# The last add of a windowed-ratio kernel: by an accumulating DMA issued from POOL, in place of a POOL instruction

## The chip, the cores and the metric

The kernel runs on one core of one Trainium2 chip. The metric is the device time of one execution in microseconds (us); lower is better. The core's engines are PE (TensorE), DVE (VectorE), ACT (ScalarE), POOL (GpSimd) and SP (SyncE, which issues the loads and stores here). Sixteen DMA engines move the data.

## The reference

x is 2 x 128 x 128 x 192 in float32 (batch, rows, w, channels). It is group-normalised (32 groups of 6 channels, statistics over rows, w and the group), a ratio of window sums is formed from the result, and the ratio is added to x.

```python
WINDOW = (1, 5, 20)
def _L0_conv_ref(x):
    w0, w1, w2 = WINDOW
    s = box_sum(box_sum(x, 1, w0), 2, w1)
    num = box_sum(s * s, 3, w2)
    d = box_sum(box_sum(box_sum(x * x, 1, w0), 2, w1), 3, w2)
    c0 = box_sum(jnp.ones((x.shape[1],), x.dtype), 0, w0)
    c1 = box_sum(jnp.ones((x.shape[2],), x.dtype), 0, w1)
    norm = c0[:, None] * c1[None, :]
    return jnp.nan_to_num(num / (d * norm[None, :, :, None]), nan=FILL)
x = x + _L0_conv_ref(_gn(x))
```

## The kernel before

w lies on the 128 partitions. The work goes by **duos** of four rows (768 float32 per partition, 384 KB in all): 32 duos for each of the two batches, n = 0 to 63. A **step** t is two duos (768 KB). All of x stays in SBUF in the tensor `xs`, which has room for 26 steps: batch 0 lies in steps 10 to 25, and batch 1 takes steps 0 to 15. Its first ten steps fall on the area in which batch 0's first window sums were parked ("raw" sums, duos 0 to 19), and its last six on the room of batch 0's steps 0 to 5, once those have been stored.

The stages are: load batch 0 and take its statistics (0 to 60 us); then one loop over n = 0 to 63 on every engine. For a duo n:

- POOL `centre` (L271): xc = x - mean, run four duos ahead.
- ACT squares xc (L309); PE makes the window sums over w, `U` from the squares and, from duo 20 on, `S` from xc (both L392); ACT copies or squares them out of PSUM (L317, L324, L337); PE makes the sums over channels, `D` and `N` (L401); ACT forms 1/D as `q` (L355, L361).
- DVE `quotient`: t1 (L588), N in place (L591), and `ratio` (L599). `ratio` has two buffers, so L599 of duo n waits until duo n-2 has been added to x.
- POOL `finish` (L277): x += ratio, in SBUF, for n = 0 to 62. The last duo is added by DVE (L659).
- SP stores a step when both of its duos are added (L207); duo 62 and duo 63 have a store each (L221, L223).

PE, ACT, DVE and POOL hold to an order written out by hand; each engine and each DMA-issuing queue works strictly in that order. On SP, the order for t = 1 to 6 is: load step t of batch 1 (waits until the raw sums there are used), wait until the store of batch 0's step t-1 has landed, load step 9+t of batch 1 into the room that this frees, then wait for the adds of duos 2t and 2t+1 and store step t. So load 15, the last of those that reuse room, is issued in round t = 6.

The statistics of batch 1 are taken by DVE inside the loop, five instructions (L529) after each quotient from n = 14 on. They come in two sets. The first set covers steps 0 to 3 and 12 to 15 of batch 1, and DVE waits for these eight loads (`wait_loaded1(dve, 0)`, L650) right after quotient 14. The second set, steps 4 to 11, is waited for after quotient 20.

Of the kernel before, what the change touches and what calls it, by code (L numbers as in the profile page):

```python
# [6 lines left out]
ALU = mybir.AluOpType  # L7
# [20 lines left out]
STEP_DUOS = 2  # L28
# [22 lines left out]
XC_RING, XC2_RING, U_RING, S2_RING, Q_RING, RATIO_RING = 3, 2, 2, 4, 2, 2  # L51
# [18 lines left out]
def window_ratio_kernel(nc, x, out):  # L70
    ctx = ExitStack()
    with ctx:
        sb = lambda name, shape: ctx.enter_context(nc.sbuf_tensor(name, shape, F32))
        ps = lambda name: ctx.enter_context(nc.psum_tensor(name, [128, DUO, 512], F32))
        sem = lambda name: ctx.enter_context(nc.semaphore(name))
# [8 lines left out]
        ratio = sb("ratio", [128, RATIO_RING, DCOLS])  # L84
# [61 lines left out]
        t1_ready = sem("t1_ready")  # L146
        t2_ready = sem("t2_ready")
        ratio_ready = sem("ratio_ready")
        out_ready = sem("out_ready")
        tail_ready = sem("tail_ready")  # L150
        stored = [sem("stored0"), sem("stored1")]

# [2 lines left out]
        def batch(n):  # L155
            return n // DUOS

        def is_raw(n):
            return n < RAW_DUOS

        def x_rows(n, duos=1):

            b = batch(n)
            first = HOME[b] * STEP + (n - b * DUOS) * DROWS
            return xs[:, first:first + duos * DROWS, :]

        def x_flat(n):
            return x_rows(n).rearrange("p r c -> p (r c)")
# [6 lines left out]
        def dram_rows(t, n, duos=1):  # L175

            b = batch(n)
            first = (n - b * DUOS) * DROWS
            return t[b, first:first + duos * DROWS, :, :].rearrange("h w c -> w h c")

        def pairs(a):
            return a.rearrange("p (a b) -> p a b", b=PCOLS)

        def in_bank(bank):
            return bank[:, :, 0:PCOLS]

        def wait_loaded1(eng, j):
            eng.wait_ge(loaded1[j], 16 * SPB * len(LATE_SETS[j]))

        @block.sync  # L190
        def _(sp):

            for j in range(LOADS):
                n, duos = j * LOAD_STEPS * STEP_DUOS, LOAD_STEPS * STEP_DUOS
                sp.dma_start(x_rows(n, duos), dram_rows(x, n, duos)).then_inc(loaded0[j], 16)

            def load1(t):

                arrived = next(loaded1[j] for j, blocks in enumerate(LATE_SETS) if t // SPB in blocks)
                n = DUOS + STEP_DUOS * t  # L200
                sp.dma_start(x_rows(n, STEP_DUOS), dram_rows(x, n, STEP_DUOS)).then_inc(arrived, 16)

            def store(t):

                n = STEP_DUOS * t
                sp.wait_ge(out_ready, n + STEP_DUOS)
                sp.dma_start(dram_rows(out, n, STEP_DUOS), x_rows(n, STEP_DUOS)).then_inc(stored[t % 2], 16)  # L207

            for t in range(STEPS):
                if t < RAW:  # L210
                    sp.wait_ge(s2_ready, STEP_DUOS * (t + 1))
                    load1(t)
                if 0 < t <= STEPS - RAW:
                    sp.wait_ge(stored[(t - 1) % 2], 16 * ((t - 1) // 2 + 1))
                    load1(RAW + t - 1)
                store(t)
            for t in range(STEPS, BATCH * STEPS - 1):
                store(t)
            last = TOTAL - 1
            sp.wait_ge(out_ready, last)  # L220
            sp.dma_start(dram_rows(out, last - 1), x_rows(last - 1)).then_inc(stored[1], 16)  # L221
            sp.wait_ge(tail_ready, 1)
            sp.dma_start(dram_rows(out, last), x_rows(last)).then_inc(stored[0], 16)  # L223
            sp.wait_ge(stored[0], 16 * (BATCH * STEPS // 2 + 1))
            sp.wait_ge(stored[1], 16 * (BATCH * STEPS // 2))

        @block.gpsimd
        def _(pool):
            own = [0]

            def band(ap, conditions):

                nc.gpsimd.memset(ap, 1.0).then_inc(pool_own, 1)
                own[0] += 1
                for base, channel, pattern in conditions:
                    pool.wait_ge(pool_own, own[0])
                    nc.gpsimd.affine_select(out=ap, in_=ap, compare_op=ALU.is_ge, fill=0.0, base=base,
                                            pattern=pattern, channel_multiplier=channel)\
                      .then_inc(pool_own, 1)
                    own[0] += 1  # L240

            def banded(j, r):

                first, end = SPAN[j]
                g0, g1 = max(first, r * C), min(end, (r + 1) * C)
                f0, f1 = max(128 * j, r * C) - 128 * j, min(128 * (j + 1), (r + 1) * C) - 128 * j
                if g0 >= g1 or f0 >= f1:
                    return
                at, cols = SPAN_AT[j] + g0 - first, g1 - g0
                inside = [(g0 - 128 * j + C_HI, -1, [[1, cols]]), (128 * j - g0 + C_LO, 1, [[-1, cols]])]  # L250
                row = [(-f0, 1, [[0, cols]])] * (f0 > 0) + [(f1 - 1, -1, [[0, cols]])] * (f1 < 128)
                band(b20[:, at:at + cols], inside + row)

            band(b5[:, :], [(W_LO, -1, [[1, W]]), (W_LO, 1, [[-1, W]])])
            pool.wait_ge(pool_own, own[0])
            nc.gpsimd.memset(averager[0][:, :], 1.0 / (TRIPLES[0] * 128)).then_inc(bands_ready, 1)
            for j in range(CHUNKS):
                for r in range(PAIR):
                    banded(j, r)
            pool.wait_ge(pool_own, own[0])  # L260
            nc.gpsimd.memset(averager[1][:, :], 1.0 / (TRIPLES[1] * 128)).then_inc(bands_ready, 1)

            def centre(n):

                b = batch(n)
                if n >= XC_RING:
                    pool.wait_ge(xc2_ready, n - XC_RING + 1)
                    if not is_raw(n - XC_RING):
                        pool.wait_ge(s_ready, n - XC_RING + 1 - RAW_DUOS)
                mean = mean_c[b][:, :, :].rearrange("p r c -> p (r c)").unsqueeze(1).to_broadcast([128, DUO, PCOLS])  # L270
                nc.gpsimd.tensor_tensor(pairs(xc[:, n % XC_RING, :]), pairs(x_flat(n)), mean, ALU.subtract)\  # L271
                  .then_inc(xc_ready, 1)

            def finish(n):

                pool.wait_ge(ratio_ready, n + 1)
                nc.gpsimd.tensor_tensor(x_flat(n), x_flat(n), ratio[:, n % RATIO_RING, :], ALU.add)\  # L277
                  .then_inc(out_ready, 1)

            for j in range(LOADS):  # L280
                pool.wait_ge(loaded0[j], 16)
            pool.wait_ge(mean_ready, 1)
            for n in range(CENTRE_AHEAD):
                centre(n)
            for n in range(TOTAL - 1):
                m = n + CENTRE_AHEAD
                if m == DUOS:
                    for j in range(len(LATE_SETS)):
                        wait_loaded1(pool, j)
                    pool.wait_ge(mean_ready, 2)  # L290
                if m < TOTAL:
                    centre(m)
                finish(n)
# [216 lines left out]
        def _(dve):  # L510
# [72 lines left out]
            def quotient(n, before_ratio=None):  # L583

                dve.wait_ge(q_ready, n + 1)
                if n:
                    dve.wait_ge(ratio_ready, n)
                nc.vector.scalar_tensor_tensor(pairs(t1[:, :]), in_bank(D), -TINY, pairs(q[:, n % Q_RING, :]),  # L588
                                               ALU.add, ALU.mult).then_inc(t1_ready, 1)
                dve.wait_ge(n_ready, n + 1)  # L590
                nc.vector.scalar_tensor_tensor(in_bank(N), in_bank(N), TINY, pairs(q[:, n % Q_RING, :]),  # L591
                                               ALU.add, ALU.mult).then_inc(t2_ready, 1)
                if before_ratio:
                    before_ratio()
                dve.wait_ge(t1_ready, n + 1)
                dve.wait_ge(t2_ready, n + 1)
                if n >= RATIO_RING:
                    dve.wait_ge(out_ready, n - RATIO_RING + 1)
                nc.vector.scalar_tensor_tensor(pairs(ratio[:, n % RATIO_RING, :]), pairs(t1[:, :]), 2.0, in_bank(N),  # L599
                                               ALU.add, ALU.mult).then_inc(ratio_ready, 1)  # L600

# [5 lines left out]
            for i, (_, c1) in enumerate(EDGES):  # L607
                ins = nc.vector.memset(coefs[:, 1 + i:2 + i], float(W_WIN - c1))
# [47 lines left out]
            n = TOTAL - 1  # L656
# [17 lines left out]
```

## Time and profile before

| | us |
|---|---|
| median of 3 runs | 412.20 (410.94 to 412.22) |
| the profiled execution | 412.27 |
| its span, first to last instruction | 410.5 |
| PE busy | 380.2 (93%) |
| ACT busy | 269.3 (66%) |
| DVE busy | 264.8 (64%) |
| POOL busy | 233.1 (57%) |

The median and the profiled execution agree within 0.1 us, so a sum made on the profile can be read against the median. Busy shares are means over stages that differ: the DMA engines are nearly always moving something up to 140 us and are a quarter busy after that, and DVE is full only between 140 and 200 us. The profile has views by stretch of time (windows), by order of time (the timeline), by who waited for whom (waits) and by line; the columns are told where rows are shown.

### The profile page before, as it was taken

To read this page: it belongs to the slowest core of one execution; us is meant where nothing else is said; L and a number is where in the kernel's file an instruction comes from. 1 tells how busy PE (TensorE), PEld (TensorE's weight loads), DVE (VectorE), ACT (ScalarE), POOL (GpSimd) and SP (SyncE) were. 2 spreads that over 40 slices of the span, in tenths; PEclk is the share of its full clock that TensorE was granted. 3 is DMA by queue.
4 is the path that set the end of the run, shared out by engine and by line. 5 is a ranking of instruction groups with operands and counts; after the bars stand their busy time and mean duration, and the time that the engine had idled before them with its cause. 6 is when DMAs were issued, how large, how long until landed. Compare 5 with 4: busy or idle time off the path is not lost. (4 is left out here: it accounts for less than half of the span.)

```text
span 410.5 us, 8111 instructions
## 1 busy us (share of the span) xinstructions
PE 380.2 (93%) x3156; PEld 375.6 (91%) x3156; DVE 264.8 (64%) x555; ACT 269.3 (66%) x353; POOL 233.1 (57%) x150
## 2 busy tenths in 40 slices
PE   1999858999999899999999999999999999999983
PEld 1999857899999889999999999999999999999982
DVE  2999863666556999999865554445555444555445
ACT  1464029887888876667666676766676776667751
POOL 4000081877777776666656667665666766666531
PEclk9999589999999999999999999999999999999997
DMA  8999002488887555222222221112222222222113
GB/s 247 327 327 321 9 0 78 131 258 258 260 249 231 157 159 154 73 77 78 78 77 78 79 78 60 50 50 73 78 78 79 77 78 78 78 77 79 52 52 128
DMA packets 66485, 50.84 MB, mean 124 GB/s; under 512 B 912, under 2 KB 66448, under 8 KB 66448
## 3 DMA queue, kind: packets, MB, share of 16 engines
q1 hardware_dynamic: 66448, 50.34, 40.2%
q8 instruction: 25, 0.41, 0.4%
q14 instruction: 12, 0.10, 0.1%
HBM read 25.17 MB, written 25.17 MB: 123 GB/s over the span
## 5 line engine op out<-in xcount | busy, mean ns | idle before, releaser
L277 POOL TENSOR_TENSOR xs<-xs,ratio 128x768 f32<-128x768 f32 x63 | 114.6, 1819 | 123.2 <-DVE ratio L599 123.2
L271 POOL TENSOR_TENSOR xc<-xs,mean_c 128x768 f32<-128x768 f32 x64 | 116.4, 1821 | 46.0 <-DVE mean_c L538 46.0
L588 DVE SCALAR_TENSOR_TENSOR t<-D,q 128x768 f32<-128x768 f32 x64 | 61.2, 957 | 115.3 <-ACT q L361 115.2
L401 PE MATMUL D<-b_r,u 128*128 128x138 f32 (+2 forms) x768 | 104.4, 284 | 7.7 <-DVE t L588 6.1
L401 PEld LDWEIGHTS D<-b_r,u 128*128 128x128 f32 x768 | 96.8, 190 | 11.0 <-issue 6.1
L401 PE MATMUL N<-b_r,s 128*128 128x138 f32 (+2 forms) x768 | 103.3, 283 | 0.2 <-DVE ratio L599 0.2
L392 PE MATMUL U<-b5d,xc 128*128 128x128 f32 x768 | 97.6, 277 | 4.2 <-ACT xc L309 3.8
L401 PEld LDWEIGHTS N<-b_r,s 128*128 128x128 f32 x768 | 96.9, 190 | 0.4 <-issue 0.4
L392 PEld LDWEIGHTS U<-b5d,xc 128*128 128x128 f32 x768 | 92.2, 193 | 4.5 <-ACT xc L309 4.1
L355 ACT ACTIVATE q<-D 128x768 f32<-128x768 f32 x64 | 51.8, 809 | 42.2 <-PE D L401 42.0
L324 ACT ACTIVATE s<-S 128x768 f32<-128x768 f32 x44 | 35.7, 811 | 49.1 <-PE S L392 49.1
L591 DVE SCALAR_TENSOR_TENSOR N<-N,q 128x768 f32<-128x768 f32 x64 | 61.7, 965 | 7.5 <-PE N L401 2.3
L392 PE MATMUL S<-b,xc 128*128 128x128 f32 x528 | 66.0, 275 | 0.0
L599 DVE SCALAR_TENSOR_TENSOR ratio<-t,N 128x768 f32<-128x768 f32 x64 | 61.1, 954 | 6.0 <-DVE N L591 0.5
L392 PEld LDWEIGHTS S<-b,xc 128*128 128x128 f32 x528 | 62.5, 191 | 0.0
L361 ACT ACTIVATE q<-q 128x768 f32<-128x768 f32 x64 | 54.0, 843 | 2.0
L309 ACT ACTIVATE xc<-xc 128x768 f32<-128x768 f32 x64 | 53.3, 833 | 1.6 <-POOL xc L271 1.6
L317 ACT ACTIVATE u<-U 128x768 f32<-128x768 f32 x64 | 50.7, 793 | 1.4 <-PE U L392 1.3
L529 DVE BATCH_NORM_STATS2 ratio<-xs 128x6 f32<-128x96 f32 x256 | 41.0, 245 | 5.9 <-DMA xs<-x 5.9
L529 DVE BATCH_NORM_STATS2 late_triples<-xs 128x6 f32<-128x384 f32 x64 | 30.6, 546 | 0.0
L392 PE MATMUL S<-b,xs 128*128 128x128 f32 x120 | 16.4, 291 | 8.5 <-DMA xs<-x 8.5
L392 PEld LDWEIGHTS S<-b,xs 128*128 128x128 f32 x120 | 15.5, 206 | 8.4 <-issue 8.4
(52 smaller groups left out, 116.4 us busy)
## 6 DMA issues: line engine op xcount, KB each, us to landing
out<-xs SPq DMA_DIRECT2D x31, 768.0 KB, 3.8
xs<-x SPq DMA_DIRECT2D x8, 1536.0 KB, 14.7
xs<-x SPq DMA_DIRECT2D x16, 768.0 KB, 6.5
out<-xs SPq DMA_DIRECT2D x2, 384.0 KB, 2.6
```

Source lines behind the costliest of these rows:

```text
L271: nc.gpsimd.tensor_tensor(pairs(xc[:, n % XC_RING, :]), pairs(x_flat(n)), mean, ALU.subtract)\
L277: nc.gpsimd.tensor_tensor(x_flat(n), x_flat(n), ratio[:, n % RATIO_RING, :], ALU.add)\
L309: nc.scalar.activation(xc2[:, n % XC2_RING, :], xc[:, n % XC_RING, :], ACT.Square)\
L317: nc.scalar.activation(pairs(u[:, n % U_RING, :]), in_bank(U), ACT.Copy).then_inc(us_ready, 1)
L355: nc.scalar.activation(pairs(q[:, n % Q_RING, :]), in_bank(D), ACT.Abs_reciprocal_sqrt, bias=-TINY)\
L361: nc.scalar.activation(q[:, n % Q_RING, :], q[:, n % Q_RING, :], ACT.Square).then_inc(q_ready, 1)
L392: mm = nc.tensor.matmul(bank[:, i, chunk], rows[:, at:at + 128], weights[:, :], start=True, stop=True)
L401: mm = nc.tensor.matmul(bank[:, i, first:end], data[:, at:at + 128], b20_r[b][:, SPAN_AT[j]:SPAN_AT[j + 1]], start=j == 0, stop=j == CHUNK ...
L529: return nc.vector.bn_stats(to.rearrange("p g a b -> p (g a b)"), rows)
L588: nc.vector.scalar_tensor_tensor(pairs(t1[:, :]), in_bank(D), -TINY, pairs(q[:, n % Q_RING, :]), ALU.add, ALU.mult).then_inc(t1_ready, 1)
L591: nc.vector.scalar_tensor_tensor(in_bank(N), in_bank(N), TINY, pairs(q[:, n % Q_RING, :]), ALU.add, ALU.mult).then_inc(t2_ready, 1)
L599: nc.vector.scalar_tensor_tensor(pairs(ratio[:, n % RATIO_RING, :]), pairs(t1[:, :]), 2.0, in_bank(N), ALU.add, ALU.mult).then_inc(ratio_r ...
```

## The change

The add of `ratio` to x is no longer a POOL instruction. POOL issues a DMA from `ratio` to `xs` with an accumulating write (x += ratio), still once for each duo n = 0 to 62 and at the same place in POOL's order, behind the same wait. A DMA counts 16 on its semaphore when all of it has landed. So the one semaphore `out_ready` becomes two, `added[0]` for even and `added[1]` for odd duos. SP's stores and DVE's wait for a free `ratio` buffer now wait for these. The last duo is still added by DVE.

```diff
-        out_ready = sem("out_ready")
+        added = [sem("added0"), sem("added1")]
@@ store(t)
-                sp.wait_ge(out_ready, n + STEP_DUOS)
+                for m in range(n, n + STEP_DUOS):
+                    sp.wait_ge(added[m % 2], 16 * (m // 2 + 1))
                 sp.dma_start(dram_rows(out, n, STEP_DUOS), x_rows(n, STEP_DUOS)).then_inc(stored[t % 2], 16)
@@ the store of duo 62
-            sp.wait_ge(out_ready, last)
+            sp.wait_ge(added[(last - 1) % 2], 16 * ((last - 1) // 2 + 1))
@@ finish(n)
                 pool.wait_ge(ratio_ready, n + 1)
-                nc.gpsimd.tensor_tensor(x_flat(n), x_flat(n), ratio[:, n % RATIO_RING, :], ALU.add)\
-                  .then_inc(out_ready, 1)
+                pool.dma_start(x_flat(n), ratio[:, n % RATIO_RING, :], accum_op=ALU.add).then_inc(added[n % 2], 16)
@@ quotient(n)
                 if n >= RATIO_RING:
-                    dve.wait_ge(out_ready, n - RATIO_RING + 1)
+                    dve.wait_ge(added[n % 2], 16 * ((n - RATIO_RING) // 2 + 1))
```

No instruction changes its place in any engine's order; PE and ACT have the same rows as before. On SP, in the rounds of loads and stores, the store waits for two DMA semaphores in place of POOL's (`s2_ready` is the wait for used raw sums, `stored0` and `stored1` those for a landed store):

```order
 L201 DMA xs<-x 128x8x192 [waits s2_ready]
 L201 DMA xs<-x 128x8x192 [waits stored0]
-L207 DMA out<-xs 128x8x192 [waits out_ready]
+L208 DMA out<-xs 128x8x192 [waits added1,added0]
 L201 DMA xs<-x 128x8x192 [waits s2_ready]
 L201 DMA xs<-x 128x8x192 [waits stored1]
```

The order within a round stays; what is new is that each store stands behind a transfer that was not there. At the end of SP's queue the same holds for the 22 last whole steps and for duo 62 (`tail_ready` is DVE's add of duo 63):

```order
-L207 DMA out<-xs 128x8x192 [waits out_ready] x22
-L221 DMA out<-xs 128x4x192 [waits out_ready]
-L223 DMA out<-xs 128x4x192 [waits tail_ready]
+L208 DMA out<-xs 128x8x192 [waits added1,added0] x22
+L222 DMA out<-xs 128x4x192 [waits added0]
+L224 DMA out<-xs 128x4x192 [waits tail_ready]
 L72 UNCONDITIONAL_BRANCH [waits stored1,stored0]
```

The last store still waits for DVE alone, but stands in SP's queue behind the one of duo 62.

## Rows read from the trace of the kernel before

**Rows 1.** The page: adds, centres, and DMA issues with KB and us to landing.
```profile
L277 POOL TENSOR_TENSOR xs<-xs,ratio 128x768 f32<-128x768 f32 x63 | 114.6, 1819 | 123.2 <-DVE ratio L599 123.2
L271 POOL TENSOR_TENSOR xc<-xs,mean_c 128x768 f32<-128x768 f32 x64 | 116.4, 1821 | 46.0 <-DVE mean_c L538 46.0
...
out<-xs SPq DMA_DIRECT2D x31, 768.0 KB, 3.8
...
out<-xs SPq DMA_DIRECT2D x2, 384.0 KB, 2.6
```

**Rows 2.** Waits of all engines: us in total, times, longest.
```profile
ACT xc L309 <- POOL xc L271: 1.6, 2, 0.9
```

**Rows 3.** Windows of stages: busy us of each engine, clock, DMA share, GB/s.
```profile
100.00:120.00 20.00, 18.74 (x151) 17.87 (x151) 12.56 (x14) 17.02 (x24) 15.64 (x9) 1.00 0.87 260
143.00:165.00 22.00, 20.77 (x177) 20.42 (x176) 21.29 (x35) 16.49 (x23) 15.79 (x9) 1.00 0.54 159
...
220.00:260.00 40.00, 40.00 (x347) 40.00 (x346) 20.26 (x22) 28.27 (x38) 26.18 (x16) 1.00 0.25 80
```

**Rows 4.** Timeline of SP's queue: start us, us, line, transfer; x2 merges two.
```profile
76.52 0.39 SPq L207 DMA_DIRECT2D out<-xs  x1
76.95 4.51 SPq L201 DMA_DIRECT2D xs<-x  x2
85.89 0.38 SPq L207 DMA_DIRECT2D out<-xs  x1
...
123.84 4.50 SPq L201 DMA_DIRECT2D xs<-x  x2
132.80 0.38 SPq L207 DMA_DIRECT2D out<-xs  x1
```

**Rows 5.** Windows of 1 us; the last two columns are DMA share, GB/s.
```profile
76.00:77.00 1.00, 1.00 (x10) 1.00 (x9) 0.75 (x1) 1.00 (x3) 1.00 (x2) 1.00 0.00 0
77.00:78.00 1.00, 0.92 (x8) 0.75 (x7) 0.89 (x2) 1.00 (x2) 1.00 (x1) 1.00 0.54 176
84.00:85.00 1.00, 1.00 (x11) 1.00 (x11) 0.00 (x0) 0.97 (x2) 0.96 (x1) 1.00 1.09 356
85.00:86.00 1.00, 1.00 (x10) 1.00 (x10) 0.37 (x1) 1.00 (x2) 1.00 (x2) 1.00 0.26 83
...
131.00:132.00 1.00, 1.00 (x11) 1.00 (x11) 0.00 (x0) 0.97 (x2) 1.00 (x1) 1.00 1.15 377
132.00:133.00 1.00, 1.00 (x11) 1.00 (x10) 0.47 (x1) 1.00 (x2) 1.00 (x2) 1.00 0.10 30
```

**Rows 6.** Timeline of POOL and of DVE from 73 us.
```profile
74.67 1.82 POOL L277 TENSOR_TENSOR xs<-xs,ratio 128x768 f32<-128x768 f32 x1 [0.81 <-DVE ratio L599]
...
78.37 0.95 DVE L599 SCALAR_TENSOR_TENSOR ratio<-t,N 128x768 f32<-128x768 f32 x1
...
83.01 0.95 DVE L599 SCALAR_TENSOR_TENSOR ratio<-t,N 128x768 f32<-128x768 f32 x1
...
87.75 0.95 DVE L599 SCALAR_TENSOR_TENSOR ratio<-t,N 128x768 f32<-128x768 f32 x1
```

**Rows 7.** Timeline of DVE at duos 14 and 15.
```profile
134.66 0.95 DVE L599 SCALAR_TENSOR_TENSOR ratio<-t,N 128x768 f32<-128x768 f32 x1
135.53 2.39 DVE L529 BATCH_NORM_STATS2 late_triples<-xs 128x6 f32<-128x384 f32 x5
137.84 0.94 DVE L588 SCALAR_TENSOR_TENSOR t<-D,q 128x768 f32<-128x768 f32 x1
```

**Rows 8.** Timeline of DVE in the long stage.
```profile
239.74 0.95 DVE L599 SCALAR_TENSOR_TENSOR ratio<-t,N 128x768 f32<-128x768 f32 x1
...
245.31 0.95 DVE L599 SCALAR_TENSOR_TENSOR ratio<-t,N 128x768 f32<-128x768 f32 x1
...
250.88 0.95 DVE L599 SCALAR_TENSOR_TENSOR ratio<-t,N 128x768 f32<-128x768 f32 x1
```

**Rows 9.** Timeline of PE after a pause; a window before it.
```profile
44.00:48.00 4.00, 3.37 (x17) 3.23 (x17) 4.00 (x27) 0.00 (x0) 0.00 (x0) 0.50 0.00 0
...
55.01 2.93 PE L392 MATMUL U<-b5d,xc 128*128 128x128 f32 x12 [1.97 <-ACT xc L309]
...
58.93 1.58 PE L392 MATMUL U<-b5d,xc 128*128 128x128 f32 x12 [0.35 <-ACT u L317]
...
138.92 1.68 PE L401 MATMUL D<-b_r,u 128*128 128x138 f32 x12 [0.81 <-DVE t L588]
```

**Rows 10.** Timeline at the end of the program.
```profile
402.07 1.82 POOL L277 TENSOR_TENSOR xs<-xs,ratio 128x768 f32<-128x768 f32 x1 [3.55 <-DVE ratio L599]
...
403.91 0.37 SPq L221 DMA_DIRECT2D out<-xs  x1
...
407.56 0.37 SPq L223 DMA_DIRECT2D out<-xs  x1
```

## The prediction

> **What bounds the kernel now.** I read the windows by stage first. From 220 us on PE is busy for all of every window, POOL for 26 of 40 us, and the DMA engines for a quarter [rows 3]; a duo takes 5.57 us, the distance of the `ratio` starts [rows 8]. Between 143 and 165 us DVE is the full engine (21.3 of 22 us), because it takes the statistics of batch 1 between the quotients. Before that, at 100 to 120 us, PE is at 18.7 of 20 us, and the DMA engines are busy for 87% at 260 GB/s [rows 3]: here each pair of duos has one store and two loads. A duo takes 4.69 us there (78.37 to 87.75 is two) [rows 6]. So POOL's adds bound nothing, and the first question is who waits for POOL, the second what room the DMA engines have while they are 87% busy.
>
> **What the removed instruction is worth.** 63 adds of 1.82 us are 114.6 us of POOL [rows 1], but the only compute engine that waits for POOL in the loop is ACT for a centred duo, 1.6 us in two waits [rows 2]. Freeing POOL can give back 1.6 us at most, and those are at the beginning, where no add stands before the centre. I put the gain at 0.
>
> **What the DMA takes from issue to landing (L).** The trace has no accumulating DMA and none issued by POOL. A store of 384 KB lands 2.6 us after its issue and one of 768 KB 3.8 us [rows 1]. The accumulating one writes 384 KB and has to read both `ratio` and x, so its movement and landing take 2.6 to 3.8 us. In front of that POOL has to make the descriptors: at the least what SP's issue takes, 0.4 us [rows 4], and I bound it above by a POOL instruction over the same elements, 1.8 us [rows 1]. L is 3.0 to 5.6 us; I take 4.5, near the middle, since nothing speaks for either end.
> The Trainium skill, "DMA: Bandwidth & Descriptors", section "Anatomy of one DMA", gives for a DMA issued by GpSimd 2.0 us plus the bytes over 436 GB/s, which would be an estimated 2.9 us for 384 KB; no row here shows such a DMA, and by that figure the sum below would be 1.6 us smaller.
>
> **Does the buffer of `ratio` come free in time?** L599 of duo n waits for the landing of duo n-2. From the end of one `ratio` to the start of the next but one there are 9.38 - 0.95 = 8.4 us in the stage of loads [rows 6] and 11.14 - 0.95 = 10.2 us later [rows 8]. Alone, 4.5 us fit in both. What hides L is thus the second buffer; with L above 8.4 (or 10.2) us the cover is gone and every further us costs half a us per duo. POOL itself has 4.69 us per duo for a centre of 1.82 us and the issue, so up to 2.9 us for an issue are free.
>
> **What is queued behind the DMA: stores, then loads.** Here is the one place that I expect to pay. SP's store of step t waits for the landing, and load 9+t waits for the store of step t-1. Step 0 is the example: POOL's add starts at 74.67, the store is issued at 76.52 [rows 4, 6]. With the DMA it is issued at 74.67 + 4.5 = 79.2, 2.65 us later. The DMA engines begin that work about 0.9 us after the issue (77.45) and are done with store, load and load at 85.3 [rows 5], 7.9 us of work in a round of 9.38 us (76.52 to 85.89 [rows 4]). Six such rounds end with load 15, issued at 123.84 + 4.50 - 0.58, near 127.8, where 0.58 is one issue of SP, and landed at 132.1 [rows 4, 5]. Check: 77.45 + 5 x 9.38 + 7.9 = 132.2.
> DVE needs load 15 at 135.53, for the first statistics instruction after quotient 14 [rows 7]. The slack is 3.4 us.
>
> **What the adds take from the DMA engines (c).** They run on the same 16 engines. At the round's own pace (7.9 us for three transfers of 768 KB) 384 KB cost 1.3 us, and 2.6 us if both reads count. The best single windows move 356 to 377 GB/s in place of the round's mean of 300 [rows 5]; an add counted once at that pace would be 1.06 us. So c is 1.06 to 2.6 us. I take 1.7 us: the reads count double, but they are rows of 3 KB within SBUF instead of rows of 768 bytes from the other memory, and some of it can slip in while the loads wait.
> The Trainium skill, "Collectives: The Full Stack", on the reduce-scatter step, says that an add inside the DMA costs the second source read, which halves the rate; it would put c at 2.6 us and the sum at 440 us. No row here shows it.
>
> A round then holds 7.9 + 2 x 1.7 = 11.3 us of work in 9.38 us of time, the engines never run dry, and the loads fall behind by about 2 us per round. From the start of step 0's store at 77.45 + 2.65 = 80.1 there are six rounds of 7.9 us, 47.4 us, and the adds of duos 2 to 14, 13 x 1.7 = 22.1 us. Load 15 lands at 80.1 + 47.4 + 22.1 = 149.6, and DVE stands still from 135.5 until then: **14.1 us**. PE, ACT and POOL run out of work within one duo, since D of duo 16 waits for t1 of duo 15. Nothing takes this up again: until 165 us DVE is full, and after that PE is [rows 3].
>
> **Restart of PE.** After the pause PE finds a lower clock: 0.50 of full speed (1.2 GHz) is the row at 44 to 48 us, where it worked with gaps, and the U box at 55.01 took 2.93 us, the next one at full speed (2.4 GHz) 1.58 [rows 9]. One to three boxes at the low level cost 1.4 to 4.2 us. D of duo 16 had waited 0.81 us for DVE anyway [rows 9], so some of it is hidden. I take **1.5 us**.
>
> **The second set and the tail.** From t = 7 on a round has one load and one store, two thirds of the work, so load 9 has time; the second set costs 0. In the tail the add of duo 62 starts at 402.07, its store would be issued at 406.6 instead of 403.91, still ahead of the last store at 407.56 [rows 10]. The last store is not held up until L exceeds 5.5 us, but the two share the engines: at most the 1.3 us of 384 KB, I take **0.4 us**.
>
> Sum: 14.1 + 1.5 + 0.4 = 16.0, and 412.3 + 16.0 = **428.3 us** (against the profiled execution, which is the median within 0.1 us).
>
> **Rivals.**
> *Hidden after all (same).* The loads get out of the way: the engines take the adds in the time in which the loads wait for the other memory, and c as seen by the loads is small. The round has 1.5 us of idle time, and of the 3.4 us of slack at load 15 L has taken 2.65, so 0.75 are left. That is enough if 2c stays under 1.5 us plus a sixth of 0.75, c under 0.8 us. For: the windows above 350 GB/s show that more can be moved than the mean. Against: these windows belong to the same busy stretch, which is at a share of about 1 nearly throughout. Time 412.3 to 413.
> *The adds set the pace (much slower).* The DMA is slow by itself, L over 10.2 us or over 5.57 us of engine time each, because reading, adding and writing back don't overlap or because POOL makes descriptors slowly. For L = 12 us a duo takes (12 + 1)/2 = 6.5 us: 0.9 us more on 44 duos and 1.8 us more on 16, 70 us, 480 us; at L = 10.5 us only the stage of loads feels it much and the time is near 440 us. For it: no row shows such a DMA. Against: the plain ones are at a quarter of the limit.
> *Faster.* Only ACT's 1.6 us are to be had [rows 2]; POOL would have to centre sooner at the loop's start, and load 15 would have to land in time (L under 3.5 us, c under 0.8 us). 410.7 us.
> *The change doesn't do what it says*: POOL issues, but holds on until the DMA has landed. Then centring has 4.69 - 1.82 = 2.9 us for L, L = 4.5 makes the stage of loads 6.3 us per duo, and the long stage (5.57 us) 6.3 too: 0.7 x 44 + 1.6 x 16 = 56 us, near 468 us. The cause differs from the second rival's, the size is alike.
>
> **How the numbers follow.** Load 15 late, with c between 1.06 and 2.6 us: 0.66. Its own range is: low end, L 3.0 and c 1.06, start 78.6, landing 139.8, stall 4.3, and 0.7 for PE: 417 us; high end, L 5.6 and c 2.6, start 81.2, landing 162.4, stall 26.9, restart 3, tail 1.5: 444 us. Hidden: 0.13. Pace set by the adds or by a POOL that holds on: 0.17. Faster: 0.04. The range from 411.5 to 444 takes in the first two and leaves out 0.2. A difference of 0.3% (1.2 us) is about what a measurement of this kernel can tell from none: faster 0.04, same 0.13, slower 0.83.
>
> **What would show it.** In the changed profile: a wait of DVE at the first statistics instruction (L530) for a DMA into xs, of 5 to 27 us; DMA share at 1 from 80 us to the end of that wait; SP's store of step 0 near 79 us; the same 5.57 us per duo after 220 us; a PE clock of 0.5 just after the stall. The steps are wrong if `ratio` (L600) waits for a DMA in the long stage (L too small in my sum), if DVE doesn't wait at duo 14 (c too large), or if the POOL issue rows are longer than 2.9 us.

## The result, and the profile after

The changed kernel takes **430.5 us** (median of 4 runs, 427.37 to 433.27) against 412.0 us before (median of the 4 runs taken beside it): a ratio of 1.045, 95% interval 1.038 to 1.053. The forecast was 428.3 us, in a range from 411.5 to 444. The profiled execution after took 427.37 us with a span of 425.7 us, 15.2 us more than the span before.

The page after, to be held against [rows 1]: POOL's groups, and the DMA queues and issues (KB each, us to landing).

```profile
L272 POOL TENSOR_TENSOR xc<-xs,mean_c 128x768 f32<-128x768 f32 x64 | 134.2, 2100 | 46.0 <-DVE mean_c L538 46.0
L278 POOL DMA_DIRECT2D xs<-ratio x63 | 56.0, 889 | 191.2 <-DVE ratio L599 191.2
...
q0 software_dynamic: 9072, 24.78, 31.8%
...
xs<-ratio POOLq DMA_DIRECT2D x63, 384.0 KB, 4.9
out<-xs SPq DMA_DIRECT2D x31, 768.0 KB, 3.9
```

POOL's own time fell from 233 to 179 us, and ACT's wait for a centred duo is the same 1.6 us as before, so nobody gained by it. The packets of the new queue, q0, take 31.8% of the 16 engines' span: 0.318 x 425.7 / 63 = 2.15 us for each add.

Who waited, in the changed kernel, us in total, times, longest:

```profile
PE D L401 <- DVE t L588: 18.2, 9, 13.5
...
DVE late_triples L529 <- DMA xs<-x: 11.9, 1, 11.9
...
DVE ratio L599 <- DMA xs<-ratio: 6.8, 6, 1.4
```

Both DVE rows are new (L529 and L599 are the lines that the prediction calls L530 and L600). The 11.9 us is one single wait, for a load of x at the first statistics instruction of batch 1. The timelines of DVE, of SP's queue and of PE around it answer to [rows 4, 7, 9]:

```profile
135.52 0.95 DVE L599 SCALAR_TENSOR_TENSOR ratio<-t,N 128x768 f32<-128x768 f32 x1 [0.71 <-DMA xs<-ratio]
148.39 2.40 DVE L529 BATCH_NORM_STATS2 late_triples<-xs 128x6 f32<-128x384 f32 x5 [11.91 <-DMA xs<-x]
```
```profile
79.26 0.39 SPq L208 DMA_DIRECT2D out<-xs  x1
79.69 5.37 SPq L201 DMA_DIRECT2D xs<-x  x2
92.37 0.38 SPq L208 DMA_DIRECT2D out<-xs  x1
...
132.79 10.22 SPq L201 DMA_DIRECT2D xs<-x  x2
...
142.64 0.37 SPq L201 DMA_DIRECT2D xs<-x  x1
```
```profile
136.62 1.69 PE L401 MATMUL N<-b_r,s 128*128 128x138 f32 x12
151.79 3.15 PE L401 MATMUL D<-b_r,u 128*128 128x138 f32 x12 [13.49 <-DVE t L588]
154.74 1.84 PE L392 MATMUL U<-b5d,xc 128*128 128x128 f32 x12
```

The first store goes out at 79.26, where it was 76.52. The pair of loads in round 6 takes 10.22 us from the first issue to the end of the second, where it was 4.50: load 15, the second of the pair, is issued at 142.64 in place of 127.98 (the last row is a finer view of the same pair; the prediction's 127.8 took 0.58 us for an issue whose row is 0.37 us). PE stands for 13.5 us and then does its next box in 3.15 us instead of 1.68.

The loads that reuse room fall behind round by round, and this is the theory's own mark. Issue times from the timelines of SP's queue:

| load | 10 | 11 | 12 | 13 | 14 | 15 |
|---|---|---|---|---|---|---|
| after | 84.7 | 97.6 | 108.9 | 121.1 | 131.6 | 142.6 |
| before | 81.1 | 90.5 | 99.8 | 109.2 | 118.6 | 128.0 |
| late by | 3.6 | 7.1 | 9.1 | 11.9 | 13.0 | 14.7 |

That is 2.2 us more in each round in the mean. Load 15 then lands at 148.3, 16.2 us later than before.

Windows of the changed kernel, the last three columns being PE's clock, DMA share and GB/s: the stage of loads, beside the 0.87 of [rows 3], one window of the long stage, and two single microseconds in the pause.

```profile
100.00:120.00 20.00, 18.82 (x151) 17.96 (x150) 12.57 (x14) 17.01 (x24) 11.76 (x9) 1.00 1.09 293
260.00:300.00 40.00, 40.00 (x346) 40.00 (x346) 20.73 (x22) 28.04 (x36) 19.17 (x14) 1.00 0.63 149
...
140.00:141.00 1.00, 0.00 (x0) 0.00 (x0) 0.00 (x0) 0.00 (x0) 0.00 (x0) 1.00 1.09 368
142.00:143.00 1.00, 0.00 (x0) 0.00 (x0) 0.00 (x0) 0.00 (x0) 0.00 (x0) 0.50 1.16 264
```

At 140 us no compute engine does anything, and the DMA engines are full; from 80 to 148.3 us their mean share is 1.07 (the share adds up the times of the packets, so it can pass 1 where packets overlap). In the long stage PE is busy for all of the window, as before.

**Where the 15.2 us went**, by the distance of the same instructions in the two timelines:

| place | after | before | shift so far |
|---|---|---|---|
| start of `ratio` of duo 14 | 135.52 | 134.66 | 0.9 |
| first statistics instruction | 148.39 | 135.53 | 12.9 |
| t1 of duo 17 | 162.30 | 148.00 | 14.3 |
| issue of the last store | 421.87 | 407.56 | 14.3 |
| end of the span | 425.7 | 410.5 | 15.2 |

So 0.9 came before duo 14, 11.9 (rounded up in the table) is the stall, 1.4 the restart of PE, nothing came in 250 us of the long stage, and 0.9 came at the end. This is the fastest of the four executions; the one with adds by DMA in the first fifteen duos, below, shows one that took as long as the median.

### The profile page after: what moved, and what is told of

Its sections match the earlier page's. It is cut to its first block and busy times, and to the rows that moved or that the text cites. A ratio compares the mean times of both kernels' runs of the same rounds, so it can differ in the third digit from the quotient of the medians.

```text
span 425.7 us, 8142 instructions
## 1 busy us (share of the span) xinstructions
PE 383.6 (90%) x3156; PEld 379.2 (89%) x3156; DVE 264.9 (62%) x555; ACT 269.1 (63%) x353; POOL 178.8 (42%) x150
## 3 DMA queue, kind: packets, MB, share of 16 engines
q0 software_dynamic: 9072, 24.78, 31.8%
## 5 line engine op out<-in xcount | busy, mean ns | idle before, releaser
L272 POOL TENSOR_TENSOR xc<-xs,mean_c 128x768 f32<-128x768 f32 x64 | 134.2, 2100 | 46.0 <-DVE mean_c L538 46.0
L278 POOL DMA_DIRECT2D xs<-ratio x63 | 56.0, 889 | 191.2 <-DVE ratio L599 191.2
L401 PE MATMUL D<-b_r,u 128*128 128x138 f32 (+2 forms) x768 | 106.6, 288 | 18.4 <-DVE t L588 18.2
L401 PEld LDWEIGHTS D<-b_r,u 128*128 128x128 f32 x768 | 99.0, 193 | 20.9 <-issue 17.5
L392 PE MATMUL U<-b5d,xc 128*128 128x128 f32 x768 | 99.2, 280 | 2.4 <-ACT xc L309 2.4
L392 PEld LDWEIGHTS U<-b5d,xc 128*128 128x128 f32 x768 | 93.8, 196 | 2.7 <-ACT xc L309 2.7
L599 DVE SCALAR_TENSOR_TENSOR ratio<-t,N 128x768 f32<-128x768 f32 x64 | 61.1, 954 | 12.2 <-DMA xs<-ratio 6.8
L529 DVE BATCH_NORM_STATS2 ratio<-xs 128x6 f32<-128x96 f32 x256 | 41.0, 253 | 5.8 <-DMA xs<-x 5.8
L529 DVE BATCH_NORM_STATS2 late_triples<-xs 128x6 f32<-128x384 f32 x64 | 30.7, 546 | 11.9 <-DMA xs<-x 11.9
```

The costliest lines, as they stand in the source:

```text
L278: pool.dma_start(x_flat(n), ratio[:, n % RATIO_RING, :], accum_op=ALU.add).then_inc(added[n % 2], 16)
L392: mm = nc.tensor.matmul(bank[:, i, chunk], rows[:, at:at + 128], weights[:, :], start=True, stop=True)
L401: mm = nc.tensor.matmul(bank[:, i, first:end], data[:, at:at + 128], b20_r[b][:, SPAN_AT[j]:SPAN_AT[j + 1]], start=j == 0, stop=j == CHUNK ...
L529: return nc.vector.bn_stats(to.rearrange("p g a b -> p (g a b)"), rows)
```

## The experiments

The theory: the adds take DMA time and hold the stores back in the stage of loads, load 15 is late, and DVE's first set of statistics waits for it. The main rival: each add has a price of its own, at every duo. A second rival within the theory: it is the latency L in front of the stores that hurts, not the engine time c.

### Where in the program: duos 0 to 14, or 15 to 62

```diff
+        def by_dma(n):
+            return n < 15          # second run: n >= 15
```

The other duos are added by POOL's instruction, as before; the waits follow.

> The accumulating DMA is used for duos 0 to 14 alone; from duo 15 on POOL adds as before. If the cost is load 15 landing late, it is all in the first fifteen duos: 426 to 431 us, with DVE waiting some 12 us for a load of x at its first statistics instruction of batch 1, and no 0.9 us at the end. If the adds cost something at every duo (descriptors, engine time, latency), a fifteenth to a quarter of the cost is left: 413 to 417 us.

> The other half: POOL adds duos 0 to 14, the DMA duos 15 to 62. Late load: no stall at duo 14, the same 5.57 us per duo later, only the 0.9 us at the end: 412.5 to 413.5 us. Cost at every duo: 424 to 428 us.

Measured: the first fifteen alone 429.6 us (1.045, interval 1.040 to 1.049), the other forty-eight 412.8 us (1.0021, interval 1.0009 to 1.0033). Waits of the first:

```profile
DVE late_triples L544 <- DMA xs<-x: 11.9, 1, 11.9
DVE ratio L614 <- DMA xs<-ratio: 11.4, 6, 2.8
```

All but 0.8 us of the price is in the first fifteen adds, and the wait is again 11.9 us. Forty-eight adds in the long stages cost 0.8 us together. The rival of a price at every duo falls.

The profiled execution of the first run took 430.1 us, as long as the median of the changed kernel, and its duos 0 to 14 are added in the same way. So it tells where a typical execution may lose the 3 us by which it is longer than the profiled one of the changed kernel. `ratio` of duo 1 and of duo 14 in it:

```profile
73.08 0.95 DVE L614 SCALAR_TENSOR_TENSOR ratio<-t,N 128x768 f32<-128x768 f32 x1
...
138.98 0.95 DVE L614 SCALAR_TENSOR_TENSOR ratio<-t,N 128x768 f32<-128x768 f32 x1 [0.79 <-DMA xs<-ratio]
```

From duo 1 to duo 14 it takes 138.98 - 73.08 = 65.9 us. The kernel before takes 134.66 - 73.64 = 61.0, the profiled execution of the changed kernel 135.52 - 73.76 = 61.8. So here 4.9 us are lost before duo 14, in the waits of `ratio` for the adds, and then the same 11.9 us at the statistics and 1.5 at PE's restart. An execution of median length thus pays twice: for late loads, and for adds that land too late for the second buffer. Why these waits are longer in one execution than in another isn't shown.

### Engine time with less latency, and accumulating against copying

The kernel before, POOL's adds kept. In front of each of the adds 0 to 12, POOL also issues a DMA that reads x of duo n+2 and writes into a spare buffer.

```diff
+                if n < EXTRA:
+                    pool.dma_start(extra_to[n % 2], x_flat(n + 2), accum_op=ALU.add).then_inc(extra[n % 2], 16)
                 nc.gpsimd.tensor_tensor(x_flat(n), x_flat(n), ratio[:, n % RATIO_RING, :], ALU.add)\
                   .then_inc(out_ready, 1)
```

(Not printed here: the two spare buffers, which take over the room of two small tensors and are filled with zeros at the start; POOL's wait for the DMA of duo n-2; and DVE's wait for the last of them at the statistics.) The second run leaves out `accum_op`. The third keeps it and lets SP's stores of those duos wait for `extra` too. The spare buffers hold no part of the result.

The stores don't go out as early as in the kernel before, since POOL issues the DMA ahead of its add. Counted from the start of `ratio` of duo 1, the first store is issued after 2.9 us in the kernel before, 4.3 in the first of these runs, 3.7 in the second, 5.7 in the third and 5.5 in the changed kernel. The plain copy is thus also the control for POOL's issue, its waits and this delay.

> The kernel before, POOL adds kept; beside them, for duos 0 to 12, POOL issues an accumulating DMA of 384 KB from x into a spare buffer that no store waits for. So the DMA engines get the work and the stores are not later. Eleven of these lie before load 15. With c = 1.6 us each: landing 77.4 + 47.4 + 17.6 = 142.4, stall 7 us, restart 1: 420 us. If the stores' latency L is what matters and not the engine time: 412 us.

> As the run with the spare accumulating DMA, but a plain copy (one read, one write, same bytes). If the second read makes the price, c is 0.8 us and load 15 just lands in time: 412 to 413 us. If the price goes by bytes written or by transfer, the time is the same as with the accumulating one, about 420 us.

> As the run with the spare accumulating DMA, but SP's stores of steps 0 to 6 also wait until it has landed, as they do in the changed kernel. Engine time and latency together: 2.65 us later than without that wait, stall near 9.7 us: 423 us. If latency costs nothing on top once the engines are full: 420 us.

Measured: 423.0 us (1.027, interval 1.025 to 1.029), 413.2 us (1.005, 1.001 to 1.008; ten runs from 411.4 to 417.5) and 427.0 us (1.036, 1.034 to 1.039). The queue row of the page and the wait at duo 14, first with the accumulating DMA, then with the plain copy, then with the stores waiting too:

```profile
q0 software_dynamic: 1872, 5.11, 6.4%
...
143.88 2.40 DVE L541 BATCH_NORM_STATS2 late_room<-xs 128x6 f32<-128x384 f32 x5 [8.52 <-DMA xs<-x]
```
```profile
q0 software_dynamic: 1040, 5.11, 3.1%
...
136.56 2.40 DVE L541 BATCH_NORM_STATS2 late_room<-xs 128x6 f32<-128x384 f32 x5 [1.09 <-DMA xs<-x]
```
```profile
147.32 2.40 DVE L544 BATCH_NORM_STATS2 late_room<-xs 128x6 f32<-128x384 f32 x5 [12.87 <-DMA xs<-x]
```

The packets of the same 5.11 MB take 0.064 x 421.2 / 13 = 2.07 us per DMA when they accumulate and 0.031 x 411.6 / 13 = 0.98 us when they are copied. Accumulating doubles the price (in 1872 packets against 1040), and without it the stall falls from 8.5 to 1.1 us. So the engine time of the accumulating form makes most of the stall, with only 1.4 of the 2.6 us by which the changed kernel's first store is late. The wait of the stores adds 4.3 us of stall (12.87 against 8.52) where I had expected 2.65, and the first store is only 1.5 us later by it. That went wrong in size; that the latency is paid more than once over six rounds would fit, but no run here takes it apart.

### Half of the adds, with and without their latency in front of the stores

```diff
+            return n < 15 and n % 2 == 0          # second run: n % 2 == 1
```

> Accumulating DMAs only for the even duos of 0 to 14, POOL adds all others. The store then follows POOL's add of the odd duo, so it is not issued later, and a round holds one add: 7.9 + 1.6 = 9.5 us of DMA work in 9.38 us. If engine time decides, the loads just keep up: load 15 lands near 134, no stall, 412.5 us. If every accumulating DMA costs the same, half of the stall is left: 420 us.

> Accumulating DMAs only for the odd duos of 0 to 14. The same engine time as with the even duos, but each store now waits for the landing, 2.65 us later. Load 15 lands near 137, 1 to 2 us of stall: 413 to 415 us. The difference to the run with the even duos is the price of the latency alone.

Measured: even duos 417.2 us (1.011, interval 1.009 to 1.014), odd duos 420.0 us (1.019, 1.017 to 1.021). DVE, at the first statistics instruction, for the even and for the odd duos, and the wait of `ratio` with the even ones:

```profile
DVE ratio L614 <- DMA xs<-ratio: 6.3, 4, 2.3
...
139.43 2.40 DVE L544 BATCH_NORM_STATS2 late_triples<-xs 128x6 f32<-128x384 f32 x5 [0.98 <-DMA xs<-x]
```
```profile
140.41 2.40 DVE L544 BATCH_NORM_STATS2 late_triples<-xs 128x6 f32<-128x384 f32 x5 [6.32 <-DMA xs<-x]
```

Both were forecast too low, by 5 to 6 us. With the even duos the stall is small (0.98 us), but not because the loads keep up: load 15 lands near 139.4 where I expected 134, and DVE itself comes 3 us later to duo 14 (`ratio` at 137.50 for 134.66), since `ratio` has waited 6.3 us in four waits for adds that land late. I take it that they do because they run beside a store and a load that start together; that isn't shown. With the odd duos no such wait is in the profile, and the stall is 6.3 us where I expected 1 to 2. Half of the adds cost about 30 to 45% of the whole (5.1 and 7.9 of 17.5 us). Counted from `ratio` of duo 1, load 15 has landed after 58.5 us in the kernel before, 65.9 with the even and 68.3 with the odd duos. So engine time alone makes it 7.4 us late, and the latency in front of the stores 2.4 more, by one profile of each run. The difference of the medians, 2.8 us, was to be the price of the latency alone; it isn't, since the even run pays in the waits of `ratio` and the odd one at the statistics.

### Moving DVE's wait

```diff
-SET_FROM = (14, 20)
+SET_FROM = (17, 20)
```

In the changed kernel and in the kernel before.

> The changed kernel, with DVE's wait for the first set of batch 1 moved from duo 14 to duo 17 (what is left over, 19 instructions, is done at duo 27). Load 15 landed at 148.3 in the changed kernel and duo 17 is reached near 149, so the 11.9 us of stall and the restart of PE go away; the pile at duo 27 costs some 5 to 7 us in both kernels. If the stall is all of the price, the time is that of the kernel before with the same edit plus 1 to 2 us (wait of ratio for the adds, the tail): 418 to 421 us. If the loads or the adds hold the kernel up elsewhere too, the difference to that kernel stays over 5 us.

> The kernel before with the same moved wait: nothing waits for a load here, it shows what the pile at duo 27 costs: 417 to 419 us.

Measured: 427.7 us with the DMA adds (three runs from 425.6 to 429.6; a fourth took 432.6) and 419.4 us with POOL's. The difference is 8.4 us in the medians and 423.9 - 417.4 = 6.5 in the profiled spans, not 1 to 2. Waits of the changed kernel with the moved wait, and where DVE stood:

```profile
171.55 2.40 DVE L529 BATCH_NORM_STATS2 late_triples<-xs 128x6 f32<-128x384 f32 x5 [5.02 <-DMA xs<-x]
...
DVE ratio L599 <- DMA xs<-ratio: 9.0, 9, 1.3
```

The wait at the first set is down to 1.1 us, but a wait of 5.0 us has appeared at duo 20, for the second set, and `ratio` waits 9.0 us for adds. In my sum the second set cost nothing, and so it was in the changed kernel, where the pause at duo 14 gives the DMA engines time to catch up: their share falls to 0.53 at 151 us and to 0 at 153. With the moved wait it stays at about 1 until 173 us, and the debt is called in at duo 20. The stall at duo 14 is where the overload is paid, not what causes it.

### Moving loads out of the way

Loads of batch 1's steps 4 to 9 are issued two by two in rounds 7 to 9 instead of one each in rounds 4 to 9.

```diff
+LOADS_AT = {0: (0,), 1: (1,), 2: (2,), 3: (3,), 7: (4, 5), 8: (6, 7), 9: (8, 9)}
@@ the loop over t on SP
-                if t < RAW:
-                    sp.wait_ge(s2_ready, STEP_DUOS * (t + 1))
-                    load1(t)
+                for k in LOADS_AT.get(t, ()):
+                    sp.wait_ge(s2_ready, STEP_DUOS * (k + 1))
+                    load1(k)
```

> The changed kernel, with the loads of batch 1's steps 4 to 9 taken out of rounds 4 to 6 and issued two by two in rounds 7 to 9, so that three fewer loads (2.6 us of DMA time each, 7.9 us) stand ahead of load 15. Late load, bound by the DMA engines: the stall falls from 11.9 to about 4 us and the time to 418 to 420 us. If load 15 is late because of the chain of waits (add landed, store, store landed) and not because the engines are full, the stall stays near 12 us, 428 us.

> The kernel before with the same moved loads: nobody waits for those loads there, so 412.0 us, within 0.3%, by every theory; it shows that the move costs nothing by itself (second set of statistics included).

Measured: 432.1 us (430.24 to 435.69) in the changed kernel, 411.5 us (0.9991, interval 0.998 to 1.000) in the kernel before. The control did as expected; the other did not. DVE's waits for loads there, the issue of load 15, and windows of 1 us between two rounds (the last two columns are DMA share and GB/s):

```profile
146.24 2.40 DVE L530 BATCH_NORM_STATS2 late_triples<-xs 128x6 f32<-128x384 f32 x5 [10.61 <-DMA xs<-x]
...
183.54 1.94 DVE L530 BATCH_NORM_STATS2 late_triples<-xs 128x6 f32<-128x384 f32 x4 [4.71 <-DMA xs<-x]
```
```profile
141.05 0.37 SPq L202 DMA_DIRECT2D xs<-x  x1
```
```profile
121.00:122.00 1.00, 1.00 (x11) 1.00 (x11) 0.59 (x1) 0.82 (x2) 0.00 (x0) 1.00 0.39 74
122.00:123.00 1.00, 0.94 (x9) 0.78 (x8) 0.50 (x2) 1.00 (x2) 0.26 (x1) 1.00 0.56 50
123.00:124.00 1.00, 1.00 (x10) 1.00 (x10) 0.83 (x1) 1.00 (x2) 1.00 (x2) 1.00 0.47 106
```

Three transfers fewer ahead of load 15 (issued at 141.05), and it was still issued only 1.6 us sooner; the moved loads then made a second stall at duo 20. So DMA work ahead of load 15 is not simply added up: 7.9 us less of it ought to have brought some 8 us. What came is the other case that I had named, a stall that stays near 12 us because of the chain of waits. The rounds with one load and one store took 9.6 to 10.2 us each, with the engines about half busy for 2 to 3 us between them. One more run asked whether SP's order made that chain (the lines are set against the run with the moved loads).

```diff
+                early = 4 <= t <= 6
+                if early:
+                    store(t)
                 if 0 < t <= STEPS - RAW:
                     sp.wait_ge(stored[(t - 1) % 2], 16 * ((t - 1) // 2 + 1))
                     load1(RAW + t - 1)
-                store(t)
+                if not early:
+                    store(t)
```

> The changed kernel with the loads of steps 4 to 9 moved out of rounds 4 to 6, and in those rounds the store of step t issued as soon as its adds have landed, ahead of the wait for the store before it and of load 9+t. The run with the moved loads alone still stood 10.6 us at duo 14 while the DMA engines were half idle near 122 us: each round was a chain (store lands, load 9+t and the next store issued together, the store lands 9 us later). If that chain is what kept load 15 late there, it is issued near 134 in place of 141.05, the stall falls to 3 to 5 us and the time to 424 to 427 us (the 4.7 us at duo 20 and a second restart of PE stay). If the engines' time alone decides, nothing changes: 431 to 433 us.

Measured: 432.0 us (430.77 to 437.1). SP's queue in rounds 5 and 6 of that run, and DVE's wait:

```profile
130.82 0.37 SPq L209 DMA_DIRECT2D out<-xs  x1
131.24 0.57 SPq L202 DMA_DIRECT2D xs<-x  x1
140.44 0.37 SPq L209 DMA_DIRECT2D out<-xs  x1
...
147.77 2.40 DVE L534 BATCH_NORM_STATS2 late_triples<-xs 128x6 f32<-128x384 f32 x5 [12.07 <-DMA xs<-x]
```

Nothing was gained. The store of each round now goes out when its own add has landed, and that is no sooner than the landing of the store before it: store, load and the two adds that run beside them all end together, 9 us after they began, about one period of two duos. SP's order is not the cause. By what was expected of the two runs, the first speaks for the chain and the second for the engines' time; together they don't settle it. Why a load, a store and two adds take 9 us together, when load and store alone take 4.5 us [rows 4] and an add occupies the engines for about 2.1, stays open: 4.5 + 2 x 2.1 = 8.7 would fit if nothing overlaps, but then the rounds with three transfers should take 7.9 + 4.2 = 12.1 us, and they took about 10.5 (121.66 to 132.09 in the changed kernel). A part of this is in the shares: the 7.9 us of the kernel before are at a mean share of 1.0, the 10.5 us at 1.10, and 12.1 / 1.10 = 11.0 us is an estimate from these rows that comes within half a us. I didn't try it with other sizes.

## Why the prediction was right

**What bounds the kernel, and that POOL's time is worth nothing:** held. 54 us less of POOL left ACT's wait for it at 1.6 us, and the time didn't fall.

**L, 4.5 us:** held with idle DMA engines. Step 0's store went out at 79.26, forecast 79.2, and from 192 us on the median from issue to landing is 4.5 us. In the stage of loads it is 8.0, up to 9.1: the sum used one L for both. The 2.9 us estimated from the Trainium skill ("DMA: Bandwidth & Descriptors", "Anatomy of one DMA") was too low for this DMA; the trace disagrees by 1.7 us against the time from the start of POOL's add in the kernel before to the store's issue (79.26 - 74.67 = 4.6), and no accumulating DMA of the changed kernel landed in less than 3.9 from its issue. For the plain copies of the same size it is near: the fastest landed in 2.6.

**The buffer of `ratio`, put at nothing:** held in the long stage (no wait there) and failed in the stage of loads. There L reached the 8.4 us of cover: six waits, 6.8 us in all. I had called the cover sufficient with the L of an idle queue. In the profiled execution only 0.7 of the 6.8 us reached the start of duo 14's `ratio`; in the run with adds by DMA in the first fifteen duos, which took as long as the median, it was 4.9 of 11.4. The sum has no term for it, and that the profiled execution hardly missed it is luck.

**c, 1.7 us, and the landing of load 15 at 149.6:** landed at 148.3, stall 11.9 for 14.1. Worked backwards, (148.3 - 80.2 - 47.4) / 13 = 1.6 us per add, and (143.8 - 78.6 - 47.4) / 11 = 1.6 in the run with spare accumulating DMAs, whose first store went out 1.15 us later than in the kernel before. By themselves the adds occupy the engines for 2.1 us, so the loads feel about three quarters of it. By the Trainium skill ("Collectives: The Full Stack", "The bandwidth ceiling: the fold count and why AG ≠ RS ≠ AR") the second source read of an add halves the rate. The runs agree with the ratio (2.07 against 0.98 us, though they don't show the reads themselves); a c of 2.6 us and 440 us they don't bear out.

**The model behind the landing time**, work added up until load 15, gave the right number in the changed kernel, and there the loads do fall behind by the 2 us per round that it says (2.2 measured). It gave the wrong number when I used it on other mixes: 420 us for 432 with the moved loads, 412.5 and 414 for 417.2 and 420.0 with half of the adds, and no price at duo 20. The step that failed in all of them is the same: that a round's time is 7.9 us per three transfers plus a constant per add. It was fitted to rounds of two loads and a store, and the landing time in the changed kernel came out right partly because that is the mix there.

**Restart, 1.5 us:** measured 1.4 (D of duo 16 also waited, so not all of it need be the clock). PE's clock stood at 0.50 from 142 us on, and its first box took 3.15 us for 1.68, the second 1.84 for 1.50.

**The tail, 0.4 us:** measured 0.9. The store of duo 62 was issued at 421.42 and the last at 421.87, so they ran side by side.

**The sum:** 16.0 us forecast and 15.2 in the profiled execution, with errors that cancel: 2.2 us less of stall, 0.9 more before duo 14, 0.5 more at the end.

**The rivals:** that the DMA engines would hide it falls by the stall itself, with a share of 1.09 at 100 to 120 us. That the adds set the pace came true in small in the stage of loads, by the waits of `ratio`. In the long stage it falls by the unchanged 5.57 us. POOL doesn't hold on until the landing: its issue row is 0.89 us.

The medians differ by 18.5 us and the profiled spans by 15.2. The changed kernel's runs spread over 6 us (427.4 to 433.3), while the kernel before and the run with adds from duo 15 on stay within 1.8 us. The overload alone doesn't make the spread: with the spare accumulating DMAs, where DVE stalls 8.5 us, the runs lie within 1.3 us, and with the plain copies, where it stalls 1.1, within 6.1. The account above is that of the fastest of its four runs. The slower ones have no trace here; the run with adds by DMA in the first fifteen duos suggests that they lose the rest before duo 14, in the waits of `ratio`, and not in a longer stall.

## What to carry to other kernels

Moving work from an idle compute engine to the DMA engines is free only where these have time: read their share by stage, not over the whole span (in the kernel before 0.01 from 41 to 62 us, 0.86 from 77 to 133, 0.54 from 143 to 165 and about a quarter from 220 on). A wait that a store takes on is also taken on by every load behind it in the queue, so look for the last load that reuses the stored room, and for who needs it and with what slack: here 3.4 us. A buffer that covers the latency of a transfer on idle engines need not cover it on full ones: here 4.5 us became 8. If the add must go by DMA, use it only in the stages with free DMA time: from duo 15 on it cost 0.8 us, in the first fifteen duos it cost 17.5.

## What the runs showed of the hardware that I had not expected

- An accumulating DMA of 384 KB from SBUF to SBUF occupies the 16 engines for 2.1 us, a plain copy of the same bytes for 1.0 us. The fastest landed 3.9 and 2.6 us after their issue, and POOL's issue row is 0.88 us for the first and 0.56 for the second. Alone on the engines (76 to 79 us, between the loop's start and the first store) it shows as 0.64 + 1.07 + 0.47 = 2.2 us, with up to 197 GB/s of the bytes written:

```profile
76.00:77.00 1.00, 1.00 (x10) 1.00 (x9) 0.63 (x1) 1.00 (x3) 1.00 (x1) 1.00 0.64 120
77.00:78.00 1.00, 0.93 (x8) 0.75 (x7) 0.89 (x2) 1.00 (x3) 0.75 (x1) 1.00 1.07 197
78.00:79.00 1.00, 1.00 (x11) 1.00 (x10) 0.91 (x2) 1.00 (x3) 0.00 (x0) 1.00 0.47 85
```

- The POOL instruction that follows such an issue shows a longer row: the centre is 2.12 us in place of 1.82, and its row begins 0.62 us after the issue's, which lasts 0.88. POOL's busy time thus fell by 54 us and not by 115.

```profile
79.74 0.88 POOL L278 DMA_DIRECT2D xs<-ratio  x1 [1.99 <-DVE ratio L599]
80.36 2.12 POOL L272 TENSOR_TENSOR xc<-xs,mean_c 128x768 f32<-128x768 f32 x1
```

- A store and a load of 768 KB issued together, beside two accumulating DMAs, took 9 us (the run with the store first); without them the store lands and the next load is issued 4.5 us after [rows 4].
